# One program block, a new order of work and slot clears behind the third f in a conditioning, routing and expert kernel

## Chip, core and metric

One core of one Trainium2 chip runs the whole kernel in one launch. The metric is the device time of the launch in microseconds (us); lower is better.

## What is computed

The input `x` has 4 batches of 512 tokens with 512 channels, `fside` (called f here) has the same shape, and `cond` gives one time factor `tf` for each batch. Cut to what matters:

```python
# conditioning, used twice (c = 0 on x, c = 1 on x2), k = v = f
ek = exp(min(k, 30)); ekv = ek * v
num = forward_scan(ekv) + backward_scan(ekv) - ekv + exp(min(u + k, 30)) * v
den = forward_scan(ek) + backward_scan(ek) - ek + exp(min(u + k, 30))
r = sigmoid(x) * num / max(den, 1e-8) * (0.8 + 0.2 * tf)
# gated recurrence: three 512x512 products, a scan over tokens, a fourth product
inp, decay, gate = silu(r @ W_in + b), sigmoid(r @ W_decay + b), sigmoid(r @ W_gate + b)
x2 = x + (gate * scan(decay, inp)) @ W_out + b_out
# second conditioning of x2 gives r2; then 8 experts, the best 2 for each token
probs = softmax(r2 @ Wg); a token takes a slot of its expert while it has any (640 each)
out = x2 + sum over its experts of prob * (relu(r2 @ w1[e]) @ w2[e])
```

## The kernel before

The program has two parts. `conditioning_and_routing` works through the four batches b = 0 to 3 and writes each token's row of `r2`, with its probabilities and number, into the `slots` of its two experts in DRAM. `experts` then reads each expert's 640 slot rows, multiplies by `w1` and `w2` and adds the weighted rows to the output. Each part has a `Block` of its own, so that all five engines leave the first before any enters the second.

The first part is 16 units (`UNITS`), each a conditioning c of a batch b for half of the channels p. A unit goes through ScalarE (`own`, `first_sums`, `first_reciprocal`), VectorE (`backward` and `fold`, four scans each; `complete`, `ratio`), GpSimd (`products`, `own_add`, `newton`) and one DMA (`own_add`, a transfer on GpSimd's queue that adds 512 KB to the sums in SBUF, where `newton` waits for it). TensorE transposes f and x (`transpose_f`, `transpose_x`), makes the gate products (`gate`), the fourth product (`project`; for the last batch tile by tile, `project_tile`), turns the results back to rows (`x2_row`, `r2_row`, `r2_tile`) and makes the routing products (`logits`, `places`). VectorE does the routing itself (`select`, `place`), and GpSimd sends the rows to their slots (`dispatch`, eight indirect DMAs for a batch).

The order in each engine's program is written out by hand, and each engine works in its order. Around the change these matter:

- The SP queue (`sync`) issues f(0) in two halves, x(0), f(1), the four weights W, `Wg`, x(1), then three clears of slots, then f(2), then five more clears, then f(3). `clear_slots` writes 1302.5 KB of an empty row for each expert; one more such clear goes from GpSimd's queue. `f_rows` and `x_rows` are single buffers, so each load waits until the last one has been transposed.
- TensorE's order has `transpose_f(2, 0)` between `transpose_x(1, 0)` and `transpose_x(1, 1)`. ScalarE's `copy_x(1, 1)` stands ahead of `first_reciprocal(1)` and `first_sums(2)`, on which VectorE's `fold(2)` waits.
- ScalarE's `r2_row(b, 0)` overwrites the row buffer, so from b = 1 on it waits for the DMAs of `dispatch(b - 1)`. On ScalarE `r2_row(2, 0)` stands ahead of the last gate tile of batch 3, `gate_sigmoid(3, 11)`.
- ScalarE's first three operations wait for ten small loads of vectors and `cond`. Its table of functions is changed by table loads, some by an explicit `exponentials()`, some put in by the compiler.

The second part: `first_turn` transposes the five tiles of 128 slot rows, ScalarE and VectorE split them in a high and a low part (`xh`, `xl`), and then TensorE runs, for each of 8 experts, a loop over 16 tiles of hidden columns with `up` (three products for each channel tile) and `down` (three for each slot tile). At the end of an expert ScalarE scales the even and VectorE the odd output tiles into `y`, each counts once for all of its tiles (`s_ya`, `s_yv`), and GpSimd adds the five tiles to the output with five indirect DMAs.

Of the kernel before, what the change touches and what calls it, by code (L numbers as in the profile page):

```python
# [20 lines left out]
ALU = mybir.AluOpType  # L21
# [4 lines left out]
B, T, C = 4, 512, 512  # L26
# [50 lines left out]
def build_program(nc, x, fside, cond, w1c, u1c, W_in, b_in, W_decay, b_decay, W_gate, b_gate,  # L77
# [3 lines left out]
    with ExitStack() as ctx:  # L81
# [9 lines left out]
        with ExitStack() as early:  # L91
# [6 lines left out]
            *(f"first_rows_in_{i}" for i in range(ST - 1)))]  # L98
        with ExitStack() as phase:
            conditioning_and_routing(nc, phase, ident, counts, rows, cond_buffers, place0, load_sems,  # L100
# [3 lines left out]
        with ExitStack() as phase:  # L104
            experts(nc, phase, ident, counts, rows, place0, load_sems, slots, out_rows, w1, w2)
# [16 lines left out]
def conditioning_and_routing(nc, ctx, ident, counts, rows, cond_buffers, place0, load_sems,  # L122
# [3 lines left out]
    def sb(name, shape, dt=F32):  # L126
        return ctx.enter_context(nc.sbuf_tensor(name, shape, dt))

    def ps(name, shape, dt=F32):
        return ctx.enter_context(nc.psum_tensor(name, shape, dt))  # L130

    def sem(name):
# [92 lines left out]
    s_own, s_num, s_scan, s_added = (  # L225
        sem("numerator_own_term"), sem("numerator_scans"), sem("denominator_scans"), sem("denominator_own_term"))
    s_first = sem("first_sums_scaled")
    s_vt = sem("vectors_transposed")
# [6 lines left out]
    s_route, s_shift, s_pexp, s_sel, s_pos, s_dest, s_count = (  # L235
        sem("route_steps"), sem("shift_ready"), sem("prob_exp"), sem("sel_ready"), sem("pos_done"), sem("dest_ready"), sem("count_done"))
# [9 lines left out]
    block = ctx.enter_context(nc.Block())  # L246
# [5 lines left out]
    @block.sync  # L252
    def _(sp):
# [57 lines left out]
    @block.gpsimd  # L311
    def _(pool):
# [29 lines left out]
        def own_add(u):  # L342
# [3 lines left out]
            pool.dma_start(sums[r][:, :, 0], eukv[:, r], accum_op=ALU.add).then_inc(s_own, 16)  # L346

        def newton(u):
# [4 lines left out]
            pool.wait_ge(s_own, 16 * (u + 1))  # L353
# [20 lines left out]
        products(0)  # L374
        products(1)
        ek_products(0, 1)
# [13 lines left out]
        own_add(4)  # L390
        products(5)
# [1349 lines left out]
```

## Time and profile before

| | us |
|---|---|
| median of 3 runs | 1160.13 |
| lowest and highest | 1153.53 and 1160.57 |
| the profiled execution | 1158.18 |
| its span | 1156.4 |
| first part, to the first transposes of slot rows | 387.3 |
| from there to the first expert product | 7.2 |
| experts, to the end of the last `y` tile | 747.2 |
| the last scatters and the end | 14.7 |

Busy shares of the span are PE 90%, its weight loads 71%, DVE (VectorE) 56%, ACT (ScalarE) 46%, POOL (GpSimd) 24%. In the first part TensorE and VectorE both work nearly all the time from 80 us on; in the second TensorE alone does. The profile's times are from the start of the span, and a wait is named after what ended it.

### The profile page before, as it was taken

The numbers are of one execution on the slowest core, as the hardware profiler recorded it, in microseconds if no ns is written. First come the engines' busy times: TensorE is split into PE (matmuls) and PEld (weight loads), VectorE is DVE, ScalarE is ACT, GpSimd is POOL, SyncE is SP. The second block draws the span as 40 slices with busy tenths as digits, with TensorE's granted clock in tenths as the row PEclk, the third lists the DMA queues.
The fourth block names the chain that finished last, engine by engine and source line by source line (L and its number), as shares of the span: only waits on it lengthen the run. The fifth ranks groups of instructions, "written<-read, shape, count | busy, mean of one in ns | idle before, by whom it ended". The sixth has DMA issues, their size and how long they took to land.

```text
span 1156.4 us, 16933 instructions
## 1 busy us (share of the span) xinstructions
PE 1035.7 (90%) x5024; PEld 817.9 (71%) x5025; DVE 643.5 (56%) x948; ACT 531.0 (46%) x848; POOL 278.9 (24%) x233
## 2 busy tenths in 40 slices
PE   2269899899977499999999999999999999999994
PEld 1134354445445499989998999898898888999893
DVE  3859999999975233343334333445554444334553
ACT  6746758667744133342334233445444334333543
POOL 3635746745555200011002000200203002000302
PEclk9999999998978699999999999999999999999997
DMA  5992134242243522244225321552645226122721
GB/s 176 300 304 64 19 93 127 37 109 64 65 129 130 201 73 73 73 136 100 73 73 141 96 73 73 148 161 99 188 145 174 109 73 154 73 74 89 209 73 22
DMA packets 67759, 132.64 MB, mean 115 GB/s; under 512 B 4983, under 2 KB 6043, under 8 KB 67737
## 3 DMA queue, kind: packets, MB, share of 16 engines
q1 hardware_dynamic: 54512, 106.58, 26.6%
q0 software_dynamic: 13008, 25.52, 11.5%
q10 hardware_dynamic: 216, 0.28, 0.1%
q8 instruction: 10, 0.16, 0.1%
q14 instruction: 13, 0.10, 0.0%
HBM read 91.99 MB, written 35.22 MB: 110 GB/s over the span
## 4 chain that ended last, share of the span: by engine, by line
PE 61%; issue 2%; ACT 1%; DVE 1%; DVEq 1%; POOL 0%; ACTq 0%; POOLq 0%
PE ps_y L1542 10%; PE ps_y L1543 10%; PE ps_y L1544 10%; PE ps_h L1522 10%; PE ps_h L1523 10%; PE ps_h L1524 10%; PE ps_t L1492 2%; POOL out_dram L1471 0%; ACT xh L1637 0%; ACT y L1644 0%; DVE hl L1699 0%; DVEq L1582 0%; PE ps_y L1485 0%; ACT w1h L1609 0%; DVE w1l L1660 0%
## 5 line engine op out<-in xcount | busy, mean ns | idle before, releaser
L1522 PE MATMUL ps_h<-xh,w1h 128*128 128x320 f32 (+3 forms) x768 | 247.2, 322 | 8.1 <-DVE hl L1699 3.8
L1524 PE MATMUL ps_h<-xh,w1l 128*128 128x320 f32 (+3 forms) x768 | 243.2, 317 | 0.0
L1523 PE MATMUL ps_h<-xl,w1h 128*128 128x320 f32 (+3 forms) x768 | 243.1, 317 | 0.0
L1471 POOL DMA_INDIRECT out_dram<-y,token x40 | 64.1, 1602 | 658.9 <-ACT y L1644 488.3
L1699 DVE SCALAR_TENSOR_TENSOR hl<-ps_h,hh 128x320 fp32r<-128x320 f32 (+1 forms) x192 | 106.9, 558 | 194.1 <-ACT hh L1633 189.5
L1542 PE MATMUL ps_y<-w2h,hh 128*128 128x512 f32 x528 | 206.5, 391 | 1.9 <-DVE hl L1699 1.9
L1543 PE MATMUL ps_y<-w2h,hl 128*128 128x512 f32 x528 | 206.7, 392 | 0.0
L1544 PE MATMUL ps_y<-w2l,hh 128*128 128x512 f32 x528 | 206.1, 390 | 0.0
L1633 ACT ACTIVATE hh<-ps_h 128x320 fp32r<-128x320 f32 (+1 forms) x192 | 94.3, 491 | 230.9 <-PE ps_h L1524 230.7
L1663 DVE TENSOR_TENSOR w2l<-raw,w2h 128x512 fp32r<-128x512 f32 x128 | 88.5, 692 | 196.8 <-ACT w2h L1612 196.8
L1612 ACT ACTIVATE w2h<-raw 128x512 fp32r x128 | 80.8, 631 | 211.5 <-PE ps_y L1544 211.5
L484 PE MATMUL ps_mm<-ratios,wm 128*128 128x512 f32 x372 | 168.4, 609 | 5.2 <-DVE xT L1179 2.9
L1522 PEld LDWEIGHTS ps_h<-xh,w1h 128*128 128x128 f32 x768 | 145.0, 189 | 16.3 <-issue 6.7
L1523 PEld LDWEIGHTS ps_h<-xl,w1h 128*128 128x128 f32 x768 | 145.2, 189 | 4.9
L1524 PEld LDWEIGHTS ps_h<-xh,w1l 128*128 128x128 f32 x768 | 145.0, 189 | 2.6
L484 PEld LDWEIGHTS ps_mm<-ratios,wm 128*128 128x128 f32 x372 | 71.0, 195 | 91.7 <-issue 86.2
L1544 PEld LDWEIGHTS ps_y<-w2l,hh 128*128 128x128 f32 x528 | 99.1, 188 | 21.3
L1542 PEld LDWEIGHTS ps_y<-w2h,hh 128*128 128x128 f32 x528 | 99.2, 188 | 20.6 <-issue 2.8
L1543 PEld LDWEIGHTS ps_y<-w2h,hl 128*128 128x128 f32 x528 | 99.2, 188 | 17.1
L1660 DVE TENSOR_TENSOR w1l<-raw,w1h 128x512 fp32r<-128x512 f32 x128 | 88.4, 691 | 16.3 <-ACT w1h L1609 12.4
L1609 ACT ACTIVATE w1h<-raw 128x512 fp32r x128 | 79.8, 624 | 0.0
L1122 DVE TENSOR_TENSOR_SCAN sums_even<-ps_decay,sums_even 128x511 f32<-128x511 f32 x32 | 38.3, 1259 | 21.7 <-ACT sums_even L763 21.6
(208 smaller groups left out, 1156.3 us busy)
## 6 DMA issues: line engine op xcount, KB each, us to landing
raw<-in_L_ffn_w_dram SPq DMA_DIRECT2D x64, 1024.0 KB, 7.1
slots<-r_rows SPq DMA_DIRECT2D x8, 1302.5 KB, 20.2
rows<-slots SPq DMA_DIRECT2D x8, 1302.5 KB, 8.1
rows<-in_x_dram SPq DMA_DIRECT2D x4, 1024.0 KB, 6.4
sums_even<-eukv POOLq DMA_DIRECT2D x8, 512.0 KB, 5.1
sums_odd<-eukv POOLq DMA_DIRECT2D x8, 512.0 KB, 5.4
out_dram<-rows SPq DMA_DIRECT2D x4, 1024.0 KB, 5.1
f_rows<-in_fside_BxSxS_dram SPq DMA_DIRECT2D x3, 1024.0 KB, 6.7
```

What stands on the lines that cost most here:

```text
L484: last = nc.tensor.matmul(ps_mm[:, k % 3, :], wm[:, m, dt, e * P:(e + 1) * P], ratio_of(0, b)[:, dt], start=(dt == 0), stop=(dt == CT - 1))
L1522: nc.tensor.matmul(o, w1h[:, j, dt, :], xh[:, dt, lo:hi], start=(dt == 0), stop=False)
L1523: nc.tensor.matmul(o, w1h[:, j, dt, :], xl[:, dt, lo:hi], start=False, stop=False)
L1524: last = nc.tensor.matmul(o, w1l[:, j, dt, :], xh[:, dt, lo:hi], start=False, stop=(dt == CT - 1))
L1542: nc.tensor.matmul(ps_y[:, i, :], hh[:, j, tok], w2h[:, j], start=first, stop=False)
L1543: nc.tensor.matmul(ps_y[:, i, :], hl[:, j, tok], w2h[:, j], start=False, stop=False)
L1544: return nc.tensor.matmul(ps_y[:, i, :], hh[:, j, tok], w2l[:, j], start=False, stop=last)
L1612: a.activation(w2h[:, (j + 1) % 2], raw2[:, bass.ds((c + (j + 1) // FC) % 2, 1), (j + 1) % FC] .rearrange("p o n -> p (o n)"), ACT.Copy).t ...
L1633: a.activation(hh[:, j % 2, lo:hi], ps_h[:, bank, 0:hi - lo], ACT.Relu).then_inc(s_hh, 1 if wide else 2)
L1660: v.tensor_tensor(w1l[:, j % 2], raw1[:, bass.ds((c + j // 2) % 2, 1), :, (j + 2) % FC * P:((j + 2) % FC + 1) * P] .rearrange("p o t q -> ...
L1663: v.tensor_tensor(w2l[:, (j + 1) % 2], raw2[:, bass.ds((c + (j + 1) // FC) % 2, 1), (j + 1) % FC] .rearrange("p o n -> p (o n)"), w2h[:, ( ...
L1699: v.scalar_tensor_tensor(out=hl[:, j % 2, lo:hi], in0=ps_h[:, bank, 0:hi - lo], scalar=0.0, in1=hh[:, j % 2, lo:hi].bitcast(F32), op0=ALU.max,
```

## The change

All engines' programs of both parts now stand in one `Block`: each engine goes from its first to its second program without a barrier. SP loads f(2) ahead of all eight clears and x(0) only when the vectors are in. Each `y` tile counts by itself, and each of the five scatters waits for its own tile. TensorE makes 30 products that nobody reads, after its last product of the first part and ahead of the transposes of the slot rows. GpSimd clears `y` after the token copy instead of before it. The own-term semaphore is split in two, by odd and even units. ScalarE loads its exp and ln table first of all. The written orders of TensorE, ScalarE, VectorE and GpSimd are new ones over the same operations. The core of the diff:

```diff
+        act.preload_act_table_set("natural_log_exp_and_others")
         act.dma_start(vec_cond[:], ...)
...
+        sp.wait_ge(s_vec, 16 * N_VEC)
         load_x(0)
...
         load_x(1)
-        sp.wait_ge(s_template, 2)
-        clear_slots(1, NE // 2)
         sp.wait_ge(s_f_tp, 2 * CT)
         load_f(2)
-        clear_slots(NE // 2, NE + 1)
+        sp.wait_ge(s_template, 2)
+        clear_slots(1, NE + 1)
...
 # TensorE
         transpose_x(1, 0)
-        transpose_f(2, 0)
         transpose_x(1, 1)
         transpose_x(1, 2)
+        transpose_f(2, 0)
+        transpose_x(1, 3)
...
         r2_row(2, 1)
-        r2_row(2, 2)
         project_tile(0)
-        r2_row(2, 3)
         project_tile(1)
         places(2)
+        r2_row(2, 2)
         project_tile(2)
+        r2_row(2, 3)
         project_tile(3)
...
+        x2_row(3, 3)
+        places(3)
         r2_tile(1)
...
 # VectorE
         fold(12)
+        select(1, routing[1])
         ratio(11)
...
         backward(14)
-        select(1, routing[1])
+        place(1, routing[1])
         fold(14)
         complete(14)
         ratio(13)
         backward(15)
-        place(1, routing[1])
         second_out(2)
+        fold(15)
         decay_inputs(3)
-        fold(15)
...
 # GpSimd
         newton(13)
+        dispatch(1, 0, 2)
         products(15)
+        dispatch(1, 2, 4)
         own_add(14)
+        own_add(15)
         newton(14)
-        dispatch(1, 0, 2)
-        dispatch(1, 2, 4)
-        own_add(15)
         newton(15)
...
 # experts, TensorE
+        pe.wait_ge(s_count, 2)
+        pe.wait_ge(s_wl1, 2)
+        pe.wait_ge(s_wl2, 1)
+        for n in range(30):
+            nc.tensor.matmul(ps_t[:].rearrange("p t q -> p (t q)"), w1h[:, 0, n % CT], w2h[:, 0], start=True, stop=True)
         for i in range(ST):
             first_turn(i)
...
 # experts, GpSimd
-            pool.wait_ge(s_ya, e + 2)
-            pool.wait_ge(s_yv, e + 2)
             for i in range(ST):
+                if i % 2 == 0:
+                    pool.wait_ge(s_ya, Y_EVEN * (e + 1) + i // 2 + 1)
+                else:
+                    pool.wait_ge(s_yv, Y_ODD * (e + 1) + i // 2 + 1)
```

## Rows read from the trace of the kernel before

**Rows 1.** Windows: PE, PEld, DVE, ACT, POOL busy, granted clock, DMA share, GB/s
```profile
100.00:200.00 100.00, 92.62 (x295) 45.61 (x294) 95.76 (x109) 68.32 (x93) 55.16 (x43) 0.97 0.27 72
200.00:300.00 100.00, 94.76 (x276) 48.26 (x275) 97.39 (x90) 71.29 (x95) 57.52 (x45) 0.93 0.31 77
335.00:346.00 11.00, 5.72 (x13) 3.26 (x14) 5.32 (x24) 5.66 (x7) 3.44 (x3) 0.50 0.35 73
398.00:1139.00 741.00, 733.85 (x4034) 656.18 (x4034) 325.03 (x523) 289.85 (x514) 60.79 (x50) 1.00 0.35 108
```
**Rows 2.** Timeline, 40 to 72 us: start, length, instruction, idle time before it
```profile
42.77 3.43 SPq L270 DMA_DIRECT2D slots<-r_rows  x3
...
46.24 5.29 SPq L255 DMA_DIRECT2D f_rows<-in_fside_BxSxS_dram  x1
...
48.36 1.12 PE L460 MATMUL ps_x<-ident,rows 128*128 128x128 f32 x4 [5.18 <-DMA rows<-in_x_dram]
...
66.89 1.12 PE L449 MATMUL ps_f<-ident,f_rows 128*128 128x128 f32 x4 [17.41 <-DMA f_rows<-in_fside_BxSxS_dram]
...
68.89 0.60 ACT L778 ACTIVATE xT<-ps_x 128x512 f32<-128x512 f32 x1 [16.11 <-PE ps_x L460]
...
71.75 4.80 DVE L1122 TENSOR_TENSOR_SCAN sums_even<-ps_decay,sums_even 128x511 f32<-128x511 f32 x4 [16.44 <-ACT sums_even L763]
```
**Rows 3.** Lines: one of ScalarE's four early table loads
```profile
L770 ACT ACT_TABLE_LOAD x1 | 1.3, 1283 | 0.0
```
**Rows 4.** Line L346, own_add's landing: issued at 76.8, then at 92.6
```profile
DMA to landing us min/median/max: 11.6/11.6/11.6
...
DMA to landing us min/median/max: 5.0/5.0/5.0
```
**Rows 5.** Timeline, 320 to 360 us, the last batch's products and what delays them
```profile
320.91 2.41 POOL L365 DMA_INDIRECT slots<-r_rows,dest  x1 [1.96 <-DVE dest L1243]
...
338.26 0.60 ACT L839 ACTIVATE r_rows<-ps_to 128x512 f32<-128x512 f32 x1 [11.62 <-DMA slots<-r_rows,dest]
...
339.54 0.69 DVE L1174 TENSOR_TENSOR z_gate<-z_gate,z_in 128x512 f32<-128x512 f32 x1 [4.03 <-ACT z_gate L800]
...
342.31 5.87 PE L536 MATMUL ps_mm<-z_gate,wm 128*128 128x512 f32 x8
...
348.45 3.60 PE L536 MATMUL ps_x<-z_gate,wm 128*128 128x512 f32 x8
...
359.39 0.75 DVE L1191 SCALAR_TENSOR_TENSOR xT<-ps_mm,vec,xT 128x512 f32<-128x512 f32 x1 [0.50 <-PE ps_mm L536]
```
**Rows 6.** Timeline, 370 to 395 us: last dispatches, slot rows, first expert product
```profile
370.99 0.98 POOL L365 DMA_INDIRECT slots<-wm,dest  x1 [4.13 <-DVE dest L1243]
...
382.65 2.25 SPq L308 DMA_DIRECT2D rows<-slots  x5
...
387.29 1.94 PE L1485 MATMUL ps_y<-ident,rows 128*128 128x128 f32 x8 [16.86 <-PEq L99]
...
391.60 1.34 DVE L1677 TENSOR_TENSOR xl<-ps_y,xh 128x512 fp32r<-128x512 f32 x2 [0.16 <-ACT xh L1618]
...
394.49 0.49 PE L1522 MATMUL ps_h<-xh,w1h 128*128 128x320 f32 x1 [2.90 <-issue]
```
**Rows 7.** Line L308: from issue to landing of the five slot tiles
```profile
DMA to landing us min/median/max: 2.7/4.0/4.4
```
**Rows 8.** Windows around the first expert product, columns as in group 1
```profile
391.20:394.70 3.50, 0.60 (x4) 0.36 (x3) 1.75 (x4) 0.97 (x2) 0.00 (x0) 0.99 1.00 356
394.70:398.00 3.30, 3.30 (x14) 3.30 (x14) 0.00 (x0) 0.05 (x1) 0.00 (x0) 0.50 0.95 331
```
**Rows 9.** Timeline, the end: even output tiles, first two of five scatters
```profile
1139.81 1.26 ACT L1644 ACTIVATE y<-ps_y,gate 128x512 f32<-128x512 f32 x2 [0.33 <-PE ps_y L1544]
...
1142.55 1.58 POOL L1471 DMA_INDIRECT out_dram<-y,token  x1 [51.04 <-DVE y L1714]
1144.43 1.54 POOL L1471 DMA_INDIRECT out_dram<-y,token  x1 [0.30 <-issue]
```

More of the change, by code:

```diff
@@ L103, in build_program, with _ @@
                                      decay_bias, w2c, u2c, Wg, w1, w2)
-        with ExitStack() as phase:
-            experts(nc, phase, ident, counts, rows, place0, load_sems, slots, out_rows, w1, w2)
+        second = experts(nc, ctx, ident, counts, rows, count_sem, place0, load_sems, slots, out_rows, w1, w2)
+        block = ctx.enter_context(nc.Block())
+        @block.sync
+        def _(sp):
+            first["sync"](sp)
+            second["sync"](sp)
+        @block.gpsimd
+        def _(pool):
+            first["gpsimd"](pool)
+            second["gpsimd"](pool)
+        @block.tensor
+        def _(pe):
+            first["tensor"](pe)
+            second["tensor"](pe)
+        @block.scalar
+        def _(act):
+            first["scalar"](act)
+            second["scalar"](act)
+        @block.vector
+        def _(dve):
+            first["vector"](dve)
+            second["vector"](dve)
 def load_chunk(sp, sem, raw1, raw2, w1, w2, e, c):
@@ L990, in _ @@
         gate_sigmoid(2, 9)
+        first_sums(12)
         gate_sigmoid(2, 10)
         gate_sigmoid(2, 11)
[L993 to L994 removed]
         r2_row(1, 0)
         copy_x(3, 0)
+        r2_row(1, 1)
+        copy_x(3, 1)
+        exponentials()
         first_reciprocal(11)
[L998 to L1000 removed]
         copy_x(3, 2)
@@ L1038, in _ @@
         r2_row(2, 1)
+        first_reciprocal(15)
+        probabilities(2)
         r2_row(2, 2)
-        first_reciprocal(15)
-        r2_row(2, 3)
-        probabilities(2)
         sigmoid_tile(0)
@@ L1056, in _ @@
         x2_row(3, 3)
+        probabilities(3)
+        r2_row(3, 0)
+        r2_row(3, 1)
+        r2_row(3, 2)
+        r2_row(3, 3)
         act.wait_ge(load_sems[0], 32)
@@ L1289, in _ @@
         fold(7)
+        ratio(6)
+        backward(8)
         complete(7)
         place(0, routing[0])
-        ratio(6)
-        backward(8)
+        fold(8)
         ratio(7)
+        complete(8)
         decay_inputs(1)
@@ L1297, in _ @@
         products_y(1)
-        fold(8)
+        backward(9)
         first_out(2)
-        complete(8)
-        backward(9)
+        fold(9)
+        complete(9)
         residual(1)
-        fold(9)
         ratio(8)
-        complete(9)
         backward(10)
+        ratio(9)
+        second_out(1)
         fold(10)
-        ratio(9)
+        complete(10)
         backward(11)
-        complete(10)
-        second_out(1)
         fold(11)
+        ratio(10)
+        backward(12)
         complete(11)
@@ L1643, in body, with vector_program @@
                 for i in range(0, ST if wide else ST - 1, 2):
-                    last = a.activation(y[:, i], ps_y[:, i, :], ACT.Copy, scale=gate[:, i:i + 1])
-                last.then_inc(s_ya, 1)
+                    a.activation(y[:, i], ps_y[:, i, :], ACT.Copy, scale=gate[:, i:i + 1]).then_inc(
+                        s_ya, 2 if i == ST - 3 and not wide else 1)
             by_width(act, e, body)
-    @block.vector
-    def _(dve):
+    def vector_program(dve):
         v = nc.vector
```

342 lines of the change are left out of this document (168 added, 174 removed).

## Prediction

> **What bounds the kernel now.** I read the windows first. In the second part TensorE is busy 733.85 of 741 us at the full clock (1.00, which is 2.4 GHz) [rows 1], and the change takes nothing out of that loop. So whatever it brings must come from the first part, from the passage between the parts, or from the end. In the first part VectorE is busy 95.76 and 97.39 of two windows of 100 us, and TensorE 92.62 and 94.76 of them [rows 1]. There an earlier start is kept, since all that follows moves with it, but a new order can win at most VectorE's own idle time, 4.2 and 2.6 us.
>
> Next the timeline, for the holes. The largest is at 55 to 72 us. SP issues three clears at 42.77 and f(2) only at 46.24, behind them, so f(2) lands at 66.89 [rows 2]. The reader is to follow the wait down three engines: TensorE waits 17.41 us for f(2), with the transposes of x(1) behind it; ScalarE waits 16.11 for one of these, with `first_sums(2)` behind it; VectorE waits 16.44 for that and starts `fold(2)` at 71.75 [rows 2]. The second hole is at 335 to 346 us. `dispatch(1)` starts at 320.91, ScalarE's row copy waits 11.62 for it until 338.26, the last gate tile stands behind, VectorE waits 4.03 for that tile, and TensorE, with 5.72 busy of 11 us, falls to the half clock (0.50, which is 1.2 GHz) [rows 1, 5]. The last products of the first part run at it: eight records take 5.87 us and the next eight, at the full clock, 3.60 [rows 5].
>
> Third the passage. The slot loads are issued from 382.65 on, TensorE starts at 387.29, held by its own sequencer at the end of the block, and the first expert product is at 394.49 [rows 6]. At the end ScalarE's tiles are done at 1139.81 + 1.26 = 1141.07, VectorE's later, and the first of five scatters starts at 1142.55, the next 1.88 behind it [rows 9].
>
> **The change part by part.**
>
> *A, f(2) and the start.* f(2) now goes out right behind x(1), with no clear ahead. The load x(1), issued just ahead of the clears, let its transpose start at 48.36 [rows 2]. A second megabyte behind it takes about 3.5 us more at the 300 GB/s or so that full DMA engines move (356 in a full window, [rows 8], is the upper bound), so f(2) is there near 50 to 52. Besides, the x tiles 1 and 2 go ahead of it on TensorE, so even a late f(2) no longer holds `first_sums(2)`. That removes 16.4 us [rows 2]. ScalarE also loses four table loads of 1.283 us, 5.1 in all [rows 3], and starts some 1 to 2 us earlier, since f's first transpose no longer waits for the vectors. Most of this is not kept: x(1) is loaded behind four weights and its transpose already waits 5.18 us for it [rows 2], so a faster ScalarE comes to the same load. Bounds 0 and 5.2; I take 2, near the lower end, since the weights fill the queue. Against it stand one more copy ahead of `first_reciprocal(1)` (0.60, as the one at 68.89, [rows 2]) and the own-term additions that now run beside the clears. These took 11.6 us beside clears and 5.0 without [rows 4]. `own_add(2)` took 11.6 already. `own_add(3)` is new among them, 6.6 later, of which the work on VectorE until `ratio(3)`, now behind `complete(4)`, covers most. Both together 2.4, bounds 0.6 and 7.2. A is 16.4 + 2 - 2.4 = 16.0, bounds 9 and 21.
>
> The clears themselves: eight of 1.3 MB at the same rate are some 35 us, so they are over near 85 to 90. What waits for all of them is the first `r2_row` and `dispatch(0)`, past 140, so they are hidden. They cost 1 us for each by which they ran beyond that.
>
> *B, the second hole.* `place(1)` moves ahead of `fold(14)`, `complete(14)`, `ratio(13)` and `backward(15)`, some 12 us of VectorE's work, and `dispatch(1)` is put ahead of the own additions 14 and 15. In today's times it starts near 306 instead of 320.91. Its eight indirect DMAs with `products(15)` between take some 17 us (from 320.91 to the wait's end at 338.26 it is 17.4, [rows 5]), which makes 323, while ScalarE comes to `r2_row(2, 0)` at 338.26 - 11.62 = 326.64 [rows 5]. So the wait goes, with 3 us to spare. What queues behind the dispatches on GpSimd is `products(15)`, `own_add(14)`, `own_add(15)` and both Newton steps. They are due only at `ratio(14)` and `ratio(15)`, behind the routing of batch 2, so they are covered. VectorE has the last y tile at 339.54 - 4.03 + 0.69 = 336.2, and TensorE makes the four project tiles at the full clock in 4 x 3.60 = 14.4 us with about 1 of transposes between: 351.6 instead of 359.4, when the last tile's residual starts [rows 5]. That is 7.8. Bounds: 0, if the wait stays, and 8.5.
>
> *C, the last routing.* `places(3)` goes ahead of twelve transposes, which brings `dest` some 1 us earlier, but the rows to be sent come later, behind it. The dispatches start at 370.99 [rows 6]. I take 0.5, bounds -1 and 1.
>
> *D, the passage.* Without the barrier TensorE starts with the first landed tile, 382.65 + 2.7 = 385.4. But the last of five tiles, issued at 384.5, lands 4.4 later, at 388.9 [rows 6, 7]. Behind it come four transposes (0.9), ScalarE's copy (0.6), VectorE's (0.7 and some tenths for the hand-over), so the last low part is ready near 391.3 instead of 391.60 + 1.34 = 392.94 [rows 6]. The 1.5 us from there to the first product stay. D is 1.7, bounds 0 and 2.2. The 30 unread products start when the splits of the first weights are done, near 373. The trace has no such product. By the nearest rows one takes between 0.18 us (the loop's mean, 733.85 / 4034, of fewer columns, [rows 1]) and 0.45 (3.60 / 8, [rows 5]), so 30 take 5.4 to 13.5 and end between 378.4 and 386.5. At worst they hold the first transposes 1 us, hidden by the last tile's landing. What they may give is a full clock for the first hidden tile. Today the clock is full during 391.2 to 394.7, when TensorE works only 0.60 of 3.5 us, and half during 394.7 to 398, when it works all the time [rows 8]. It falls after a pause and rises after work. The new pauses, up to 385.4 and then between arriving tiles, are as long as that one, so I take 0 for the clock, bounds 0 and 1.6 (half of the 3.3 us at the half clock, [rows 8]). The Trainium skill, page TensorE: Matmul & The Clock Gate, part 1 on the clock gate, would have sustained matmuls lift the clock and idling drop it again. By its plain reading that such a warm-up prepares what follows, the sum would be 1.6 us shorter, and the trace speaks for the other half of the rule.
>
> *E, the end.* The first scatter waits for one ScalarE tile (done 0.63 after 1139.81) instead of VectorE's second, some 1.2 us later. The five scatters follow each other at 1.88 as before [rows 9], with one more wait before each. E is 0.9, bounds 0 and 1.3. The `y` clear moved behind the token copy, the split own semaphore and the count per tile within the loop cost nothing: GpSimd is busy 60.79 of 741 us there [rows 1]. Without that cover they would cost some tenths for each expert.
>
> *The middle.* All other swaps, 140 to 320 us: I take 0, with bounds -6 (VectorE's idle time of 6.8, [rows 1], nearly all gone) and +8.
>
> **Sum.** 16.0 + 7.8 + 0.5 + 1.7 + 0.9 = 26.9. Against the profiled execution's own 1158.2 that is 1131.3. The median of the runs is 1.9 above that execution and the lowest run 4.7 below it, so I put 1131.5.
>
> **Rivals.**
> - *The wait for dispatch(1) stays* (ScalarE comes earlier than I think, or `places(1)` is late). For it: only 3 us to spare, and eight dispatches beside VectorE's work took as long as 17 us. Against it: `place(1)` moves by 12 us. B falls to 0: 1139.3.
> - *The clears choke the own additions.* Eight clears stand in one queue, and f(2) behind three took 66.89 - 46.24 = 20.6 us [rows 2]. If an addition took that instead of 11.6, `ratio(2)` and `ratio(3)` would each be late by some 6 us: 1143. Against it: `own_add(2)` ran beside clears in 11.6 [rows 4], and it comes from another queue. The Trainium skill, page DMA: Bandwidth & Descriptors, section Queues, rings and completion order, says that each DMA engine goes round-robin between its queues, packet by packet. By that rule an addition would not wait for the queued clears, and the trace agrees with its 11.6 us.
> - *A new wait in the middle.* The same form as the one at 326.64: one engine's order meets something late, for instance `select(1)`, now right behind `fold(12)`, when `logits(1)` has moved behind `r2_row(1, 2)` on TensorE. One such hole costs VectorE 4 and the half clock up to 4 [rows 5], two of them 16: about 1144 to 1147.
> - *More than I count.* The clock stays full (1.6) and the new order takes 5 of the 6.8 us idle: 1125.
> - *Slower.* One program for each engine instead of two could lay TensorE's loop so that its jumps pay for fetching instructions. It runs 8 x 8 passes. To be slower by 11.6 us it must first eat 26.9, so it decides from 38.5 / 64 = 0.60 us a pass on: 1171.7. Against it: today TensorE idles 7.15 us in all of these 741 [rows 1], 0.11 a pass, and the body is the same.
>
> **How the numbers follow.** The forecast has 0.55, its own range 1125 to 1137. The wait that stays has 0.12 (1139.3), the choked additions 0.07 (1143), the new waits 0.08 (1144 to 1147), more than counted 0.16 (1125 and a little below), slower 0.02. The range 1120 to 1141 holds the forecast, the gainful case and the first rival, and leaves out a bit less than 2 in 10. A change of 1%, 11.6 us, is about what a measurement of this kernel can tell from none. Faster by more than that means under 1148.5: 0.95. Within it 0.03, slower 0.02.
>
> **What the changed profile would show.** A: VectorE's first `fold(2)` scan near 55.7, without a wait over 5 us between 45 and 60, and a landing of f(2) under 10 us. B: ScalarE's row copy of batch 2 without a wait for DMA, no window at clock 0.50 in the last 50 us of the first part, and the first part's last dispatch 24 us earlier. D: some 4 us from the last slot tile's landing to the first expert product, which takes 0.49 as now [rows 6] if the clock is half, and clearly less if it is full. E: the first scatter 1.4 us after TensorE's last product. I would be wrong if `first_sums(2)` found another late transfer, if dispatch(1) still ended behind ScalarE, or if TensorE, with 5 to 7% idle in the middle, became the bound there and kept the second half of A.

## The result and the profile after

| | before | after |
|---|---|---|
| median of 4 runs, us | 1160.03 | 1139.26 |
| lowest and highest | 1153.53 and 1160.57 | 1138.31 and 1141.39 |
| the profiled execution's span | 1156.4 | 1136.6 |

The changed kernel takes 0.984 of the time, with a 95% interval of 0.981 to 0.988. It is faster by 20.8 us by the medians where 28.6 were forecast. By the ratio it is 18, and the later batches of the kernel before, with medians of 1156.3 to 1158.2, put it at 17 to 19. The two spans of the profiled executions differ by 19.8 us, and that is what the stages below have to add up to. In each I read how much earlier the same instruction starts than before.

| stage, at which instruction | us earlier | forecast |
|---|---|---|
| A, `fold(2)` | 19.7 | 16.0 |
| middle, TensorE's first gate product of batch 2 (203.69) | 10.2 | still 16.0 |
| B, ScalarE's row copy of batch 2 and TensorE behind it | 19.0 to 19.8 | 23.8 |
| C, first scatter of the last batch (351.98) | 19.0 | 24.3 |
| D, first expert product | 19.8 | 26.0 |
| experts, ScalarE's last `y` tile | 21.3 | 26.0 |
| E, end of the span | 19.8 | 26.9 |

Windows of the changed kernel, columns as in group 1 of before:

```profile
100.00:200.00 100.00, 87.38 (x277) 43.86 (x275) 97.27 (x110) 65.12 (x92) 65.80 (x50) 0.92 0.27 74
316.00:327.00 11.00, 10.01 (x50) 6.66 (x49) 10.96 (x11) 3.06 (x4) 5.60 (x3) 0.85 0.18 31
325.00:327.00 2.00, 2.00 (x3) 0.78 (x3) 1.96 (x4) 0.00 (x0) 0.00 (x0) 0.50 0.00 0
371.80:374.70 2.90, 0.04 (x2) 0.01 (x1) 1.58 (x4) 0.60 (x1) 1.18 (x2) 0.50 1.04 382
374.70:378.00 3.30, 3.30 (x12) 3.30 (x13) 0.00 (x0) 0.00 (x0) 0.00 (x0) 0.50 0.88 270
378.00:1118.00 740.00, 734.21 (x4037) 656.76 (x4036) 324.81 (x524) 290.17 (x514) 60.24 (x50) 1.00 0.35 108
```

The experts' loop is what it was: 734.21 busy of 740 beside 733.85 of 741 [rows 1]. The work of the hole at 335 to 346 now stands at 316 to 327, and TensorE is busy 10.01 of these 11 us instead of 5.72. The half clock has not gone with the hole: TensorE still idles 0.99 us ahead of its first project product at 323.32, and from 325 to 327 the granted clock is 0.50. The first eight project products take 5.40 us (5.87 before), the next eight 3.60 as before. From 100 to 200 TensorE works 5.2 us less than before, while VectorE shows 97.27, more than before. Work of VectorE has become longer there. Its timeline, and GpSimd's, in the changed kernel (start, length, instruction, idle time before it):

```profile
52.08 4.80 DVE L1159 TENSOR_TENSOR_SCAN sums_even<-ps_decay,sums_even 128x511 f32<-128x511 f32 x4 [2.29 <-ACT sums_even L789]
...
180.38 0.98 POOL L389 DMA_INDIRECT slots<-r_rows,dest  x1 [0.30 <-issue]
181.05 12.31 DVE L1194 SCALAR_TENSOR_TENSOR ratios<-ratios,neg_scale,sig 128x2048 f32<-128x2048 f32 x1
181.38 1.28 POOL L363 TENSOR_TENSOR eukv<-euk,kT 128x512 f32<-128x512 f32 x1
...
188.72 2.48 POOL L379 TENSOR_TENSOR sums_even<-sums_even,euk 128x512 f32<-128x512 f32 x2
...
203.69 5.67 PE L513 MATMUL ps_mm<-ratios,wm 128*128 128x512 f32 x8 [11.64 <-DVE xT L1216]
```

and the same operation of VectorE in the kernel before:

```profile
200.20 2.32 DVE L1157 SCALAR_TENSOR_TENSOR ratios<-ratios,neg_scale,sig 128x2048 f32<-128x2048 f32 x1
```

The first row answers to the 16.44 us of wait in [rows 2]: it is down to 2.29. The third is `first_out(2)`, the product of batch 2's ratios with the sigmoid. Its operands all lie in SBUF, it took 2.32 us before and 12.31 now, and it begins as GpSimd, done with the scatters of `dispatch(0)`, begins eight operations in a row. The last of these ends at 191.20, and `first_out(2)` ends 2.16 behind, at 193.36. So it seems to have done nothing until GpSimd had finished. VectorE's residual of batch 1 stands behind it, and TensorE waits 11.64 us for that. No wait shows this loss on VectorE: it is booked as busy time.

The end, in the changed kernel: ScalarE's last `y` tiles and the first two scatters in the timeline, then GpSimd's drain at the end of the block in the view of one line (its length in ns, min, median and max, then its start).

```profile
1118.51 1.26 ACT L1696 ACTIVATE y<-ps_y,gate 128x512 f32<-128x512 f32 x2 [0.33 <-PE ps_y L1588]
...
1120.03 1.57 POOL L1516 DMA_INDIRECT out_dram<-y,token  x1 [52.59 <-ACT y L1696]
1121.90 1.54 POOL L1516 DMA_INDIRECT out_dram<-y,token  x1 [0.30 <-issue]
```

```profile
L81 POOLq DRAIN  x1: 6034/6034/6034, 1130.3 to 1130.3; - x1
```

and the drains that ended the two blocks of the kernel before:

```profile
L99 POOLq DRAIN  x1: 4072/4072/4072, 382.8 to 382.8; - x1
...
L104 POOLq DRAIN  x1: 3325/3325/3325, 1152.9 to 1152.9; - x1
```

The first scatter starts 1.52 behind the start of ScalarE's row, against 2.74 in [rows 9]: 1.22 gained, as forecast. But the drain takes 2.71 us more than the one that ended the program before, and my working had no drain in it.

### The profile page after: what moved, and what is told of

It reads as the page before. It is cut to its first block, busy times and chain, and to the rows that moved or that the text cites. A ratio compares the mean times of both kernels' runs of the same rounds, so it can differ in the third digit from the quotient of the medians.

```text
span 1136.6 us, 17058 instructions
## 1 busy us (share of the span) xinstructions
PE 1045.6 (92%) x5054; PEld 824.3 (73%) x5055; DVE 653.3 (57%) x948; ACT 525.7 (46%) x844; POOL 280.9 (25%) x233
## 3 DMA queue, kind: packets, MB, share of 16 engines
q1 hardware_dynamic: 54512, 106.58, 26.9%
## 4 chain that ended last, share of the span: by engine, by line
PE 78%; DVE 6%; issue 6%; ACT 4%; DMA 2%; POOL 2%; DVEq 1%; ACTq 1%; SPq 0%; POOLq 0%
PE ps_y L1586 10%; PE ps_y L1587 10%; PE ps_y L1588 10%; PE ps_mm L513 10%; PE ps_h L1566 10%; PE ps_h L1568 10%; PE ps_h L1567 10%; PE ps_mm L530 2%; PE ps_t L1536 2%; DMA rows<-in_x_dram 1%; POOL slots L389 1%; DVE sums_odd L1159 1%; PE ps_x L530 1%; PE ps_small L600 1%; DVE ratios L1194 1%
## 5 line engine op out<-in xcount | busy, mean ns | idle before, releaser
L1588 PEld LDWEIGHTS ps_y<-w2l,hh 128*128 128x128 f32 x528 | 99.2, 188 | 21.3
L530 PE MATMUL ps_mm<-z_gate,wm 128*128 128x512 f32 x72 | 37.2, 650 | 4.1 <-DVE z_gate L1211 4.1
```

The costliest lines, as they stand in the source:

```text
L1588: return nc.tensor.matmul(ps_y[:, i, :], hh[:, j, tok], w2l[:, j], start=False, stop=last)
```

## The experiments

The theory was that `first_out(2)` is held by GpSimd's chain of operations, and that this costs most of the 9.5 us of the middle (19.7 - 10.2). Its rivals: the operation is slow for another reason (transfers beside it, its place), or the loss comes with any earlier front. Smaller questions were what each part of A and B is worth, the drain, and TensorE's clock at the start of the experts. Each kernel is the changed one with the edit shown, except e4. Beside each ratio to the kernel before stands its 95% interval; the changed kernel's own is 0.9843 (0.981 to 0.988). 0.001 of it is 1.16 us.

### Is it GpSimd's chain?

**e1**, `first_out(2)` ahead of the four scans of `backward(9)`:

```diff
         products_y(1)
-        backward(9)
         first_out(2)
+        backward(9)
```

> The changed kernel with one edit: VectorE's first_out(2) moves ahead of backward(9), so that it is no longer issued while GpSimd runs products(9), ek_products(3) and newton(8) back to back. Theory: in the changed kernel first_out(2), an operation of VectorE with every operand in SBUF, took 12.31 us instead of 2.3 because it stood beside that chain of GpSimd operations (181.38 to 191.20). Then its time falls back to about 2.3 us where GpSimd's chain has not begun, the 11.64 us in which TensorE waited for gate(2) goes to about 2, and the time falls by 8 to 10 us, to about 1130. Rival (the operation is slow wherever it stands in this kernel, for the transfers of the own additions beside it): it stays near 12 us and the time stays within 2 us of 1139. Second rival (backward(9) merely becomes the late one, since it now waits in its place beside the chain): first_out(2) is short but the residual's path gains less than 4 us.

Measured: 1131.42 us, 0.9776 (0.9758 to 0.9794).

```profile
178.01 2.35 DVE L1194 SCALAR_TENSOR_TENSOR ratios<-ratios,neg_scale,sig 128x2048 f32<-128x2048 f32 x1
...
196.45 3.96 PE L513 MATMUL ps_mm<-ratios,wm 128*128 128x512 f32 x5 [2.60 <-DVE xT L1216]
```

The operation takes 2.35 us, TensorE's wait falls from 11.64 to 2.60, and 7.8 us come back. The scans, with one operand in PSUM, then stand beside GpSimd's chain at their usual 1.20. The gates start 17.4 us earlier than before, so at that point 7.2 of the 9.5 us are back; at `first_out(3)`, which starts 20.4 us earlier than before instead of 12.7, none is missing. So the operation isn't slow wherever it stands, `backward(9)` didn't become the late one in its place, and an earlier front alone loses nothing. That it was the chain and not the place in VectorE's order, this run doesn't tell; e2 does.

**e2**, GpSimd's order changed instead, VectorE's left as it is:

```diff
         dispatch(0, 0, 2)
-        dispatch(0, 2, 4)
         products(9)
+        dispatch(0, 2, 4)
         ek_products(3, 0)
```

> The changed kernel with one edit on GpSimd's queue: the second half of dispatch(0) moves behind products(9). VectorE's order is left as it is. Theory (GpSimd's chain of operations without a gap holds VectorE's first_out(2)): products(9) runs earlier and the issue of the scatters parts it from ek_products(3) and newton(8), so first_out(2) falls to between 2.3 and about 6 us, and the time falls by 6 to 10 us. Rival (first_out(2) is slow for the transfers beside it, or for where it stands in VectorE's order): it stays near 12 us and the time within 2 us of 1139.

Measured: 1132.89 us, 0.9785 (0.9755 to 0.9815). `first_out(2)` takes 2.33. Its place in VectorE's order is the old one, so the place was not the cause. But another operation is now the victim: `complete(9)`'s sum of two SBUF operands, 1.20 in the changed kernel.

```profile
185.71 0.98 POOL L389 DMA_INDIRECT slots<-r_rows,dest  x1 [0.30 <-issue]
186.70 1.30 POOL L356 TENSOR_TENSOR ekv<-ek,kT 128x512 f32<-128x512 f32 x1
...
189.18 5.99 DVE L1166 TENSOR_TENSOR sums_odd<-sums_odd,euk 128x1024 f32<-128x1024 f32 x1
```

**e4**, in the kernel before, only f(2) ahead of the clears:

```diff
-        sp.wait_ge(s_template, 2)
-        clear_slots(1, NE // 2)
         sp.wait_ge(s_f_tp, 2 * CT)
         load_f(2)
-        clear_slots(NE // 2, NE + 1)
+        sp.wait_ge(s_template, 2)
+        clear_slots(1, NE + 1)
```

> The kernel before with one edit on the transfer queue: the third token tile's features go ahead of all clears, and nothing else changes. Theory (the front's gain belongs to this edit): the stall of 16.4 us at the third features goes, and TensorE is 14 to 17 us earlier at fold(2); and since dispatch and everything of GpSimd keep the old order behind it, the middle of the kernel loses none of it. The time falls by 13 to 17 us to 1143 to 1147. Rival (the loss in the middle comes from the front's being earlier, so that GpSimd's chain meets first_out(2) in the old order as well): first_out(2) is over 8 us and the time falls by only 4 to 8 us.

Measured: 1142.92 us, 0.9882 (0.9865 to 0.9898), 13.3 us under the kernel before.

```profile
51.42 1.11 PE L448 MATMUL ps_f<-ident,f_rows 128*128 128x128 f32 x4 [2.59 <-DMA f_rows<-in_fside_BxSxS_dram]
```

That transpose stood at 66.89 [rows 2], so it is 15.5 us earlier, and about 14 of them are left at the first expert product (380.20 instead of 394.49): in the old order of the engines `first_out(2)` takes 2.32. This one reordered load gives two thirds of the whole change by the medians, three quarters by the ratios.

### Why does it lose every turn?

One thing did not fit. In the same traces other operations of VectorE waited for one operation of GpSimd only. The Trainium skill, page SBUF — State Buffer, section SBUF: two separate sides, says that VectorE and GpSimd share a pair of ports under an exclusive lock, that VectorE's operations with two SBUF inputs need it against GpSimd's that read SBUF, and that whichever starts first keeps it for the whole instruction. A wait for one operation agrees with that; eight in a row do not follow from it.

**e11**, the one operation as four, and **e12**, a tiny write in GpSimd's chain:

```diff
-            v.scalar_tensor_tensor(out=ratio_of(0, b)[:, part], ...)
+            for part in parts:   # for b = 2 one channel tile each
+                last = v.scalar_tensor_tensor(out=ratio_of(0, b)[:, part], ...)
```

> The changed kernel with first_out(2) as four operations of 512 elements a partition instead of one of 2048, at the same place of VectorE's queue, beside the same chain of GpSimd. Theory (VectorE's operation gets nothing while GpSimd's operations follow each other without a gap, whatever its length): the first of the four ends only behind the chain, all four together end 2.5 to 3.5 us behind it, and the time is within 1.5 us of the changed kernel. Rival (only the long operation loses every turn, short ones take turns with GpSimd's as the operations of complete() did in the same trace): the four end by about 187 us, GpSimd's chain gets longer by their 2.4 us, and the time falls by 3 to 7 us.

```diff
         products(9)
+        g.memset(gap[:], 0.0)
         ek_products(3, 0)
```

> The changed kernel with one tiny operation of GpSimd between products(9) and ek_products(3): it writes 8 elements a partition that nothing reads, and reads nothing. Theory (VectorE's operation gets its turn as soon as GpSimd's chain is broken by anything that doesn't read SBUF): first_out(2) ends about 2.3 us behind that operation, near 186.5 us instead of 193.4, and the time falls by 4 to 7 us. Rival (only an idle GpSimd lets it in; the tiny operation follows and is followed without a gap): first_out(2) stays near 12 us and the time within 1.5 us of the changed kernel.

Measured: e11 1140.06 us, 0.9844 (0.9823 to 0.9864); e12 1139.72 us, 0.9842 (0.9823 to 0.9862). In e11 the first quarter took 9.51 us and the other three 0.74 each, and in e12 the whole took 12.36. My expectation for e12 was wrong: an operation that reads nothing does not let VectorE in.

I then went through the first parts of all traces for operations of VectorE that took over 0.3 us more than their shortest. In the 18 traces of this case 35 were held by two to nine operations of GpSimd, and every one of these chains stood directly behind an issue of a transfer on GpSimd's own queue. In chains that did not, none waited for more than one, though over 70 of them had two or more still to come. The converse does not hold quite: where the first operation behind such an issue had itself waited for VectorE (the `newton` at 312.70 of the changed kernel, 2.4 instead of 1.26), the two took turns, operation by operation. That is a pattern, not yet a cause, and e13 and e14 test it.

**e13** and **e14**. Both put the same extra work on VectorE, which moves `first_out(2)` into the middle of GpSimd's first operations; e13 also puts an idle gap between the last scatter and the chain:

```diff
 # e13 and e14, in backward(9), ahead of its last two scans
+                    for n in range(4):
+                        last = v.tensor_reduce(spare[:, n:n + 1], d0(b, c, ct, T), mybir.AxisListType.X, ALU.add)
+                    last.then_inc(s_gap, 1)
 # e13 alone, GpSimd
         dispatch(0, 2, 4)
+        pool.wait_ge(s_gap, 1)
         products(9)
```

> The changed kernel with two edits. On VectorE backward(9) makes four sums over a PSUM bank that nothing reads, ahead of its last two scans, about 2.4 us, so that first_out(2) starts about 2.4 us later. GpSimd waits for them between the last scatter of dispatch(0) and products(9), so that its chain starts near 182.4, some 0.9 us behind the issue of that scatter, and still ahead of first_out(2), which starts near 183.4. Theory (a chain that stands directly behind an issue of GpSimd keeps VectorE out until it ends, a chain that begins behind an idle gap lets it in after the operation that runs): first_out(2) takes 2.4 to 3.7 us and ends near 186.5, GpSimd's chain gets 2.3 us longer, and the time is 4 to 8 us under that of the run without the gap. Rival (any chain without a gap keeps it out): first_out(2) ends 2.2 us behind the chain, after 10 to 11 us, and the time is 2 to 3 us over the changed kernel.

> The control to the run before: the same four unread sums on VectorE, but GpSimd doesn't wait, so that its chain stands directly behind the last scatter of dispatch(0) again, from 181.4 on. By both theories first_out(2) starts near 183.4, is held until the chain ends near 191.3, and ends 2.2 us behind it, after about 10 us; it ends where it does in the changed kernel, so the time is within 1.5 us of that. If it is let in early here, the delayed start was what mattered and not the gap.

Measured: e13 1134.59 us, 0.9794 (0.9772 to 0.9815); e14 1140.51 us, 0.9849 (0.9829 to 0.987). With the gap (e13):

```profile
179.29 0.98 POOL L391 DMA_INDIRECT slots<-r_rows,dest  x1 [0.30 <-issue]
181.47 1.27 POOL L365 TENSOR_TENSOR eukv<-euk,kT 128x512 f32<-128x512 f32 x1 [1.20 <-DVE spare L1154]
182.70 1.27 POOL L366 TENSOR_TENSOR eukv<-euk,kT 128x512 f32<-128x512 f32 x1
183.55 2.57 DVE L1201 SCALAR_TENSOR_TENSOR ratios<-ratios,neg_scale,sig 128x2048 f32<-128x2048 f32 x1
183.93 3.31 POOL L358 TENSOR_TENSOR ekv<-ek,kT 128x512 f32<-128x512 f32 x1
```

Without it (e14):

```profile
181.24 0.98 POOL L391 DMA_INDIRECT slots<-r_rows,dest  x1 [0.30 <-issue]
182.24 1.29 POOL L365 TENSOR_TENSOR eukv<-euk,kT 128x512 f32<-128x512 f32 x1
184.29 9.92 DVE L1200 SCALAR_TENSOR_TENSOR ratios<-ratios,neg_scale,sig 128x2048 f32<-128x2048 f32 x1
```

In both, `first_out(2)` starts 2.05 to 2.08 us behind the chain's first operation. With 1.20 us of idle GpSimd between scatter and chain it is let in after the operation that runs, takes 2.57, and GpSimd's next one waits for it (3.31 instead of 1.28). Without the gap it is held to the end. The gap is worth 5.9 us, although it delays GpSimd's work. So this much is shown: the chain that stands directly behind a transfer issue of GpSimd keeps VectorE out, and the pause between them, here a wait on a semaphore, is what lets it in. How long a pause must be, and by what mechanism, these runs don't tell.

### What the parts of A and B are worth

**e3**, three clears back ahead of f(2), all else new:

```diff
+        sp.wait_ge(s_template, 2)
+        clear_slots(1, NE // 2)
         sp.wait_ge(s_f_tp, 2 * CT)
         load_f(2)
-        sp.wait_ge(s_template, 2)
-        clear_slots(1, NE + 1)
+        clear_slots(NE // 2, NE + 1)
```

> The changed kernel with one edit on the transfer queue: clears 1 to 3 go back ahead of the third token tile's features, where the kernel before had them; all else of the new order stays. Theory (in the kernel before these three clears made the third features late, and with them the fold that TensorE waited for): f(2) is issued about 5 us later and lands about 13 to 15 us later, fold(2) starts near 65 instead of 52 us, and the time rises by 8 to 16 us over the changed kernel, to 1147 to 1155. Rival (the new order of the compute engines around the third features had already made the delay harmless): within 3 us of 1139.

Measured: 1147.52 us, 0.9915 (0.9892 to 0.9937), 8.3 us more by the ratios. TensorE's transpose of f(2) waits 13.92 us for the load and starts 14.6 later than in the changed kernel. I had expected `fold(2)` near 65, and that was wrong: it starts at 52.58, against 52.08 in the changed kernel. So the new order of TensorE and ScalarE alone takes the stall off VectorE, and what the late load still holds is TensorE, whose gates stand behind the transpose: the first of them starts 13.5 us later (64.25), and 11.5 are left at 71.29 and 9.0 at the first of batch 2. The order of SP's queue is not harmless, but by another path than `first_sums(2)`.

**e9**, without `preload_act_table_set` ahead of ScalarE's queue:

> The changed kernel without the table load that stands first on ScalarE's queue; the first activation then loads its table itself. Theory (the front is set by the third features and x(1), not by when ScalarE's first table is there): one more table load of about 1.3 us falls into the first 12 us, TensorE's fold(2) starts at most 1.5 us later than 52.1 us, and the time is 0 to 1.5 us over the changed kernel. Rival (the early load sits in front of ScalarE's own transfer issues, and without it the transfers start sooner): up to 1 us faster.

Measured: 1141.72 us, 0.9868 (0.9848 to 0.9888), 2.9 us more. I had expected one more load. In fact ScalarE has 31 instead of 27: four more of 1.283 us, 5.1 in all, in the first 37 us. One early load of a table set for exponentials and logarithms together had spared them. TensorE's gates start 3.6 us later (54.37 instead of 50.79). 1.8 of these are left at the first expert product, and the ratios give 2.9 in all. So that one line gives more than I had put on ScalarE's earlier start (2 us).

**e5**, `place(1)` and `dispatch(1)` about where the kernel before had them:

```diff
 # VectorE
         backward(14)
-        place(1, routing[1])
 ...
         backward(15)
+        place(1, routing[1])
 # GpSimd
-        dispatch(1, 0, 2)
         products(15)
-        dispatch(1, 2, 4)
         own_add(14)
-        own_add(15)
         newton(14)
+        dispatch(1, 0, 2)
+        dispatch(1, 2, 4)
+        own_add(15)
         newton(15)
```

> The changed kernel with one edit: place(1) on VectorE goes behind backward(15), and dispatch(1) on GpSimd behind newton(14), about where the kernel before had them. Theory (the second gain, some 9 us around 320 to 340 us, belongs to the earlier dispatch(1)): the wait of ScalarE's r2_row(2) for TensorE turns into a wait for the transfer again and the time rises by 7 to 9 us over the changed kernel, to 1146 to 1148. Rival (the gain came from the clears having drained out of the queues, so that the scatters land sooner wherever they are issued): under 3 us.

Measured: 1142.46 us, 0.9863 (0.9846 to 0.9881), 2.3 us more by the ratios and 5.0 by the spans.

```profile
326.11 0.60 ACT L865 ACTIVATE r_rows<-ps_to 128x512 f32<-128x512 f32 x1 [11.52 <-DMA slots<-r_rows,dest]
```

The old wait of 11.62 [rows 5] is back, so the earlier dispatch is what removes it. But it costs 5 us at most, where I had expected 7 to 9 and the stage gained 8.8. One reason is a loss that the earlier dispatch brings along in the changed kernel:

```profile
312.70 4.62 POOL L376 TENSOR_TENSOR sums_even<-sums_even,euk 128x512 f32<-128x512 f32 x2
314.08 8.60 DVE L1205 TENSOR_TENSOR_SCAN z_in<-z_dec,z_in 128x512 f32<-128x512 f32 x4
317.28 4.32 POOL L379 TENSOR_TENSOR sums_even<-sums_even,euk 128x512 f32<-128x512 f32 x2
```

These four scans of the last batch have their operands in SBUF. They took 1.20 us each before and 1.19 to 1.24 in e5, and here 2.18 to 2.22, since `newton(14)` now lies beside them and the two take turns. That is 4.1 us of VectorE just ahead of the tiles that TensorE waits for at 323.32. So e5 prices the removed wait less this loss. Besides, 2.5 us of the stage's gain are there at `first_out(3)` (264.32, 12.7 us earlier than before), ahead of any dispatch of batch 1, and belong to other swaps, which I didn't take apart. The scatters also land sooner in both kernels, at the median 3.0 us behind their issue in the changed kernel and 3.2 in e5 against 4.5 before, and that did not keep the wait from coming back.

### The passage and the end

**e6**, one drain of GpSimd behind its last scatter of the first part:

```diff
         pool.wait_ge(s_disp, 16 * (1 + TT * TOPK * B))
+        pool.drain()
```

> The changed kernel with one instruction more: GpSimd drains once behind its last scatter of the first part, where it then has nothing to do until the second part's scatters. Theory (the drain at the program's end takes longer because it covers all 89 transfers of GpSimd in one block instead of 40): the last drain falls from 6.03 to about 3.3 us, and the time falls by 2 to 2.7 us. Rival (the last drain's time is that of the last scatters alone, or of the barrier): it stays near 6 us and the time within 0.5 us.

Measured: 1137.0 us, 0.9809 (0.9792 to 0.9827), 2.3 us less by the medians, 3.9 by the ratios.

```profile
L462 POOLq DRAIN  x1: 4072/4072/4072, 365.6 to 365.6; - x1
...
L81 POOLq DRAIN  x1: 3321/3321/3321, 1132.3 to 1132.3; - x1
```

The added drain takes the 4.07 us of the one that ended the first block before, where GpSimd has nothing to do, and the last falls from 6.03 to 3.32. In these traces the drain's length goes with the transfers that GpSimd has issued since the last drain: 40 take 3.32, 49 take 4.07, and 89 take 6.03 (6.36 in e5). Why, they don't tell.

**e15**, all five scatters wait for all tiles, as before:

> The changed kernel with one edit: each expert's scatters wait for all five output tiles, as in the kernel before, instead of each for its own. Theory (the count for each tile lets the first scatter go one tile of VectorE earlier): the first of the last five scatters starts 1.2 us later against ScalarE's last tile, 2.7 instead of 1.5, and the time rises by 1 to 1.3 us. Rival (the drain that follows ends at the same time anyway, since its time depends on the last scatter alone, or the waits between the scatters cost what the early start gives): within 0.3 us.

Measured: 1140.82 us, 0.9853 (0.9838 to 0.9868). The first scatter starts 1.48 us behind ScalarE's last tile as before, instead of 0.25, and the four others and the drain follow by the same steps. The trace gives 1.23 us for it and the ratios 1.2, which is within their intervals.

**e7**, without the 30 unread products, and **e8**, with 36 of them, 2 more behind each turned tile of rows and 7 behind the last:

> The changed kernel without its 30 products that nothing reads. They stand while TensorE waits for the rows anyway. Theory (TensorE's clock at the first expert products is set by what it did just before, and the 30 products end 11 us too early for them): the first expert products still run at half clock until about 378, the transposes of the rows run at half clock as well, and the time is between 0 and 1.5 us longer. Rival (they carry the clock through to the loop): over 2 us longer. Rival (they cost time, because they stand ahead of the transposes of the rows): shorter by up to 1 us.

> The changed kernel with 36 unread products instead of 30, then 2 behind each turned tile of rows and 7 behind the last, so that TensorE is busy until the first expert product. Theory (clock follows what TensorE did just before): the first expert products run at full clock, 0.24 us each instead of 0.47 until 378, and the time falls by 1 to 1.8 us. Rival (products between the transposes delay them by more than the clock gives back): 0 to 2 us longer.

Measured: e7 1141.39 us, 0.9856 (0.9839 to 0.9873); e8 1137.54 us, 0.9828 (0.9809 to 0.9846). In e8 the clock is full where the changed kernel has 0.50, and the 21st expert product starts 3.03 us behind the first instead of 4.69 (a window of e8, then its timeline):

```profile
374.80:378.00 3.20, 3.14 (x21) 3.15 (x22) 0.49 (x1) 0.44 (x1) 0.00 (x0) 1.00 0.87 292
```

```profile
380.22 0.41 PE L1566 MATMUL ps_h<-xh,w1h 128*128 128x320 f32 x1 [1.58 <-DVE hl L1753]
```

But then it waits 1.58 us for VectorE's low part of the hidden tile, which it does not do in the changed kernel. Counted from the issue of the row loads to the first `down` product it took 20.6 us in e8, 19.3 in e7 and 19.6 in the changed kernel, and with the same code there 18.3 (e15) to 20.6 (e1) in the others. So neither the unread products nor the full clock show a gain that these runs could tell from the scatter of this passage.

**e10**, e1, e6 and e8 together, and **e16**, e1 and e6 alone:

> The changed kernel with three edits that were measured one by one: first_out(2) ahead of backward(9) (7.8 us faster), GpSimd's drain behind its last scatter of the first part (2.2 us faster), and unread products up to the first expert product (within 2 us). Theory (the three gains lie at different places and add up): 1127 to 1130. Rival (the first gain makes GpSimd's last scatters end nearer to TensorE's need, so that the drain in their wake delays the rows): 1130 or more.

> The changed kernel with first_out(2) ahead of backward(9) and GpSimd's drain behind its last scatter of the first part; the 30 unread products stay where the changed kernel has them. Against the run with all three edits (1127.3) this prices the moved products. Theory (a fast start of the expert products is lost again within the first expert to the wait for hl, the low part that VectorE makes of the hidden tile): within 1 us of that run. Rival (the full clock at the first products is kept): 1.2 to 1.8 us slower than that run.

Measured: e10 1127.3 us, 0.9735 (0.9711 to 0.9758); e16 1128.15 us, 0.9744 (0.9719 to 0.977). By the ratios the gains of e1 and e6 add up, and the products bring nothing that can be measured: from the first expert product to the first `down` it is 8.47 us in e10 and 8.48 in e16. The two profiled executions of e1 and e16 can't be subtracted for the drain: e16 is 4.5 us ahead already at `first_out(3)` (252.24 against 256.69), long ahead of the added drain. Its own part is the 2.71 us by which the last drain is shorter. e16 is the changed kernel with two lines moved or added. It is 11 us faster than that and 30 us faster than the kernel before, beyond what I had forecast for the change.

## Why the prediction was right and wrong

- **A** was right in mechanism and low in size: 19.7 instead of 16.0. The stall and its removal came as worked out (e4: 15.5; f(2) is transposed at 47.86, a little before the 50 to 52 of my estimate), and also that a late f(2) no longer holds `first_sums(2)` (e3). The term of ScalarE's earlier start (2) was mis-sized. I held x(1)'s load as the end of all gain there, but SP issues it earlier too, its transpose starts 5.0 us earlier (43.35), and the missing table loads alone were worth 2.9 (e9). The own additions 2 and 3 took 11.4 and 10.1 us from issue to landing, about as I had said of additions beside clears, but the 2.4 that I took off for it is not seen: GpSimd waited 0.69 us for the second of them (83.35).
- **The middle** is the step that failed: 0 forecast, 9.5 lost, beyond the bound of +8. e1 shows that holding `first_out(2)` cost 7.2 us of it at the gates and 7.7 at `first_out(3)`. I had named a new wait there as a rival (0.08, 1144 to 1147), but as one engine's order meeting something late. No order met anything late: an operation of VectorE became five times as long, next to work of GpSimd that it has nothing to do with. From the trace of before this could have been bounded: an operation that takes 0.47 alone takes 2.82 there at 153.96, directly behind a transfer issue of GpSimd. I read durations as properties of an operation, not of what runs beside it.
- **B** came to 8.8 against 7.8, but for at most 5 of it by the mechanism I gave (e5). The wait for `dispatch(1)` went, as did VectorE's wait of 4.03. The half clock did not go: I had said that no window of the last 50 us of the first part would be at 0.50, and 325 to 327 is, so the four project tiles took not 14.4 but 16.2 us of products (5.40 and three times 3.60). Nor had I seen that `newton(14)` would come to lie beside the scans of the last batch (4.1 us). That B came near its forecast is partly luck: gains that I had not counted made up for two losses.
- **C** gave 0 instead of 0.5, inside its bounds.
- **D**: 0.8 instead of 1.7. The row loads are issued at 363.92, the last tile lands 6.4 behind (6.2 before) and the first product comes 4.4 behind that, where I had said 4. The clock was taken at 0 and is 0.50 at the first products, as forecast. The 30 products took 8.64 us, within the 5.4 to 13.5 of the bounds. Of what the experts gained, 1.4 us lie between the first expert product and the first `down` product (8.8 us instead of 10.2). They are not the change's: e4 has them too (8.7), with the old code there.
- **E**: the start of the first scatter gave 1.2 as said, and the drain took 2.7, which makes -1.5 where 0.9 stood. The barrier that I saw fall in D had its price in such a drain (4.07, ending at 386.85, just ahead of the barrier at 387.0); I counted its removal and not that one drain at the end now covers both parts.

The sum of the steps was 26.9. A gave 3.7 more, B 1.0 more, and the experts 1.5 that I had not counted. The middle took 9.5, the end 2.4, and C and D gave 1.4 less. That is 19.8, as the spans show. The range of 1120 to 1141 held the time, which lies 7.8 us over the forecast, at the place of the first rival and for none of its reasons: the wait for `dispatch(1)` did go.

## What to carry to other kernels

An order that is right for each engine by itself can still put two engines in each other's way: before moving work of GpSimd or VectorE, look at what the other has beside it, and compare the duration of one operation over all its occurrences, since such a loss is shown as busy time and not as a wait. When several changes come together, try the smallest alone first: one reordered transfer gave two thirds or more of this one. To see what became of a hole, follow its work to its new time: the same window of both profiles holds different work. When two blocks become one, ask what the end of the first had paid for.

## What the runs showed of the hardware

- An operation of VectorE with all operands in SBUF and a chain of GpSimd's operations that read SBUF exclude each other. If the chain stands directly behind one of GpSimd's own transfer issues, VectorE waits for the whole chain (12.31 us instead of 2.33, e14 9.92); behind an idle gap of 1.20 us it waits for one operation (2.57, e13). Where the first operation of the chain had itself waited for VectorE, they take turns, and scans of 1.20 us take 2.2 (`newton(14)`, 314.08). Its scans with one operand in PSUM go on beside the chain at 1.20. Cutting the operation in four or putting a small write in the chain changes nothing (e11, e12).
- In these traces GpSimd's drain is longer the more transfers it has issued since its last: 3.32 us for 40, 4.07 for 49, 6.03 for 89 (6.36 once). A drain of 4.07 in an idle place took 2.71 off the last one (e6).
- Unread products that keep TensorE busy up to the first real one keep it at full clock (1.00 instead of 0.50 in e8), and that bought nothing here, because VectorE's half of the next step became the wait.
